# A different order for the start of an attention and expert layer: where the weights are staged, and when they are multiplied together

## The chip, the cores and the metric

The kernel runs on one NeuronCore of a Trainium2 chip. The metric is the time of one execution on the device, in microseconds; the figure before is the median of three runs. The engines are TensorE (PE; PEld are its weight loads), VectorE (DVE), ScalarE (ACT), GpSimd (POOL), and SyncE (SP), which issues all loads and stores. Each works through its own list of instructions in order; semaphores tie the lists together.

## What is computed

Eight batches of 128 rows and 512 columns, all float32. Per batch b:

```python
c  = x @ cond_weight[ids_b].T                 # a 512 x 512 matrix chosen by index
q, k, v = c @ Wq, c @ Wk, c @ Wv              # 32 heads of 16, 8 groups of k and v
ctx = softmax(causal(rope(q) @ rope(k).T / 4)) @ v
x1 = x + ctx @ Wo
c2 = x1 @ W.T + (x1 @ lora_A[id2_b]) @ lora_B.T / 2
base, logits, h = c2 @ W_base.T + b, c2 @ W_router.T, c2 @ A.T
w  = softmax over the two largest logits, zero elsewhere   # 8 experts
out = x1 + base + 2 * (h * w) @ B             # rank 16 for each expert
```

The second condition and what follows it have no nonlinearity between them. So the kernel multiplies their matrices once, at the start: `fused_w` = W.T times [router | A | base], 512 x 648, and `lora_g` = lora_B.T times the same. These products are made in ten *fusing blocks*.

## The kernel before

Every matrix operand is held as two halves, `hi` (rounded to fp32r) and `lo` (what is left), and a product takes three passes: hi hi, hi lo, lo hi. For weights ScalarE makes `hi` (a copy, L402) and VectorE makes `lo` (a subtraction, `low_of`, L588); for later batches' condition matrices GpSimd makes `lo` (L346). A weight thus goes through a load into a raw buffer, ScalarE, VectorE, and only then can TensorE use it. Weights of 512 rows come in KT = 4 quarters of 128.

Rounds. The work is software-pipelined. In round t, batch f = t + 1 is at its condition, projections and rotation, batch t at scores and softmax, r = t - 1 at context, output and FFN, q = t - 2 at its experts' end. The loop runs from t = -1, and each engine has its list written out as such a loop; the order in the list is the order of execution. The steps that matter here:

- `condition(f)`: 12 matmuls (L1020 to L1022). ScalarE copies the result (`copy_c`, tile turn), `transpose_c` turns it (L938), ScalarE and VectorE split it into c_t hi and lo (`split_c`), and `project_q` and `project_kv` use it (L927, L928, L932).
- ScalarE copies v out of PSUM (`copy_v`), VectorE multiplies q and k by the rotation's tables (`rotate_k`, `rotate_q`, L705, L707), GpSimd adds the two products (`add_rotated`, L362), `transpose_qk` turns them (L1047, L938), and ScalarE and VectorE split them (`split_qk`, `split_k`, `split_q`).
- `score(t, p)`, p = 0 to 3 (L954), is the first pass of scores, of which VectorE takes the row maxima (`maxima`, 8 instructions for each p, L655). p = 2 and 3 overwrite p = 0 and 1, so they wait until the maxima of those are read. `transpose_maxima` (L964) and `spread_maxima` bring the maxima into the second, transposed pass `score_t(t, e)` (L976, L981, L986), of which ScalarE takes the exponentials (`exp_scores`, L502).
- `fuse(n)`, n = 0 to 9 (L1133 to L1135): 12 matmuls of 324 columns into one of two PSUM banks in turn, drained by `split_fused(n)` on ScalarE and then VectorE. Blocks 0 and 1 make `lora_g`, 2 to 9 `fused_w`. A block can't start before the block two before it is drained. In the kernel before, all ten stand in round 0, each between two steps of batches 0 and 1. context(0, 0) of round 1 waits for the last drain.

Weights. w_q and w_kv are loaded first, into `stage_a`. FFN's matrices (router_t, experts_a_t, base_t) go to `stage_a` too, and SyncE issues them when the last quarter of q, k, v's is split (`qkv_lo`). w2 goes to `stage_b`, then w_o to the same. SyncE's list is: ids, x_t, w_kv; condition 0; w_q, cos and sin, w2, lora_b; batch 1's condition; FFN's, bias, experts_b, w_o; then batch by batch.

The exponentials of e = 0 are written over `stage_a`, those of e = 1 into a buffer of their own (`probs_1`).

## Time and profile before

| | us |
|---|---|
| median of 3 runs (268.58 to 269.58) | 268.69 |
| the profiled execution | 269.5 |
| its span, first to last instruction | 267.7 |
| TensorE busy in it | 237.8 |
| VectorE, ScalarE, GpSimd busy | 182.6, 117.9, 86.7 |
| mean granted clock of TensorE (1.0 is 2.4 GHz) | 0.974 |

The profile page gives shares of the whole span. For a change in the first 80 us the tables by stage and the engines' own timelines say more: a timeline's row gives start, duration, engine, line, operation, tile and count, and in brackets the idle time before it and what ended that. A matmul's duration holds some 0.17 us of pipeline behind its last column; the distance from start to start is its price.

### The profile page before, as it was taken

To read this page: it belongs to the slowest core of one execution; us is meant where nothing else is said; L and a number is where in the kernel's file an instruction comes from. 1 tells how busy PE (TensorE), PEld (TensorE's weight loads), DVE (VectorE), ACT (ScalarE), POOL (GpSimd) and SP (SyncE) were. 2 spreads that over 40 slices of the span, in tenths; PEclk is the share of its full clock that TensorE was granted. 3 is DMA by queue.
4 is the path that set the end of the run, shared out by engine and by line. 5 is a ranking of instruction groups with operands and counts; after the bars stand their busy time and mean duration, and the time that the engine had idled before them with its cause. 6 is when DMAs were issued, how large, how long until landed. Compare 5 with 4: busy or idle time off the path is not lost.

```text
span 267.7 us, 5712 instructions
## 1 busy us (share of the span) xinstructions
PE 237.8 (89%) x2010; PEld 176.8 (66%) x2010; DVE 182.6 (68%) x908; ACT 117.9 (44%) x269; POOL 86.7 (32%) x92
## 2 busy tenths in 40 slices
PE   0565699999699999999999999999999999889994
PEld 0444588888376866586658765876587766556883
DVE  3583766441985689668965896589658966977653
ACT  2687233457607443643364336433642164054210
POOL 7207405322928005610562056205620050001010
PEclk9988689999989999999999999999999999999999
DMA  5999340041000700260027001600200030001111
GB/s 140 329 349 380 141 139 0 2 164 36 0 12 7 232 2 1 69 218 2 1 61 224 5 1 59 229 0 4 63 28 0 4 76 15 0 4 42 46 42 39
DMA packets 20000, 21.17 MB, mean 79 GB/s; under 512 B 6404, under 2 KB 11524, under 8 KB 19972
## 3 DMA queue, kind: packets, MB, share of 16 engines
q1 hardware_dynamic: 19972, 20.81, 24.5%
q8 instruction: 16, 0.26, 0.4%
q14 instruction: 12, 0.10, 0.1%
HBM read 18.71 MB, written 2.10 MB: 78 GB/s over the span
## 4 chain that ended last, share of the span: by engine, by line
PE 63%; DVE 20%; issue 7%; ACT 6%; SPq 1%; DMA 1%; POOL 0%; DVEq 0%
PE bank L932 9%; PE bank L927 9%; PE bank L928 8%; DVE thrown L655 7%; PE bank L1006 4%; PE bank L954 3%; PE bank L1020 3%; PE bank L1078 3%; PE bank L1021 3%; PE bank L1022 3%; PE bank L938 3%; PE bank L1133 2%; PE bank L981 2%; DVE turned L673 2%; PE bank L1134 2%
## 5 line engine op out<-in xcount | busy, mean ns | idle before, releaser
L346 POOL TENSOR_TENSOR cond_w_lo<-cond_raw,cond_w_hi 128x512 fp32r<-128x512 f32 x28 | 36.3, 1310 | 69.7 <-ACT cond_w_hi L402 69.7
L655 DVE CUSTOM_DVE_ANT_0 thrown<-bank,causal 128x128 f32<-128x128 f32 x256 | 56.0, 283 | 0.0
L362 POOL TENSOR_TENSOR rope_b<-rope_a,rope_b 128x128 f32<-128x128 f32 (+1 forms) x16 | 16.2, 1015 | 52.9 <-DVE rope_b L707 52.9
L927 PE MATMUL bank<-qkv_w_hi,c_t_hi 128*128 128x512 f32 (+1 forms) x64 | 22.5, 368 | 1.4 <-DVE c_t_lo L588 1.4
L1020 PE MATMUL bank<-cond_w_hi,xt_hi 128*128 128x512 f32 x32 | 14.7, 459 | 9.4 <-DVE cond_w_lo L588 9.4
L928 PE MATMUL bank<-qkv_w_lo,c_t_hi 128*128 128x512 f32 (+1 forms) x64 | 21.7, 355 | 0.0
L927 PE MATMUL bank<-fused_w_hi,late 128*128 128x324 f32 (+2 forms) x68 | 20.9, 322 | 0.0
L655 DVE DVE_READ_ACCUMULATOR2_ANT neg_max<- 128x1 f32 x256 | 20.6, 81 | 0.0
L371 POOL TENSOR_TENSOR x_bias<-x,bias_row 128x512 f32<-128x512 f32 x8 | 10.2, 1278 | 29.9 <-DVE out_sb L809 28.8
L928 PE MATMUL bank<-fused_w_lo,late 128*128 128x324 f32 (+2 forms) x68 | 19.9, 306 | 0.0
L402 ACT ACTIVATE cond_w_hi<-cond_raw 128x512 fp32r<-128x512 f32 x32 | 17.8, 622 | 4.0 <-DMA cond_raw<-cond_w_t 4.0
L502 ACT ACTIVATE probs<-bank 128x512 f32<-128x512 f32 x32 | 16.5, 604 | 6.6 <-PE bank L986 6.6
L402 ACT ACTIVATE turn<-bank 128x512 f32<-128x512 f32 x8 | 4.8, 598 | 31.6 <-PE bank L1022 31.5
L927 PEld LDWEIGHTS bank<-qkv_w_hi,c_t_hi 128*128 128x128 f32 x64 | 12.7, 199 | 9.0 <-issue 5.8
L502 ACT ACTIVATE stage_a<-bank 128x512 f32<-128x512 f32 x32 | 16.5, 603 | 1.1 <-PE bank L986 0.3
L402 ACT ACTIVATE v_ones<-bank 128x64 f32<-128x64 f32 x16 | 2.7, 221 | 32.0 <-PE bank L932 32.0
L402 ACT ACTIVATE late<-bank 128x128 fp32r<-128x128 f32 (+1 forms) x24 | 9.5, 397 | 16.3 <-PE bank L1100 10.6
L954 PE MATMUL bank<-k_pad_hi,q_t_hi 32*128 32x256 f32 x128 | 11.2, 339 | 5.3 <-DVE neg_max L655 3.2
L402 ACT ACTIVATE max_rows<-bank,own_p 128x128 fp32r<-128x128 f32 x32 | 9.1, 373 | 11.8 <-PE bank L964 11.8
L1020 PEld LDWEIGHTS bank<-cond_w_hi,xt_hi 128*128 128x128 f32 x32 | 6.9, 217 | 11.2 <-issue 9.6
L932 PE MATMUL bank<-qkv_w_hi,c_t_lo 128*128 128x512 f32 (+1 forms) x64 | 14.3, 346 | 0.0
L1021 PE MATMUL bank<-cond_w_lo,xt_hi 128*128 128x512 f32 x32 | 14.3, 446 | 0.0
(150 smaller groups left out, 629.8 us busy)
## 6 DMA issues: line engine op xcount, KB each, us to landing
cond_raw<-cond_w_t SPq DMA_DIRECT2D x7, 1024.0 KB, 5.5
xt_raw<-x_t SPq DMA_DIRECT2D x8, 256.0 KB, 5.9
x_nat<-x SPq DMA_DIRECT2D x8, 256.0 KB, 2.6
out<-out_sb SPq DMA_DIRECT2D x8, 256.0 KB, 2.0
cond_raw<-cond_w_t SPq DMA_DIRECT2D x4, 256.0 KB, 3.6
stage_a<-w_q SPq DMA_DIRECT2D x4, 256.0 KB, 5.3
stage_b<-w SPq DMA_DIRECT2D x4, 256.0 KB, 4.9
stage_a<-base_t SPq DMA_DIRECT2D x1, 1024.0 KB, 7.4
```

The source lines that it names most:

```text
L346: pool.tensor_tensor(cond_w.lo[:, k, :], cond_raw[:, k, :], f32(cond_w.hi[:, k, :]), ALU.subtract).then_inc(cond_lo, 1)
L362: pool.tensor_tensor(qk[:, at:at + w], rope_a[:, at:at + w], rope_b[:, at:at + w], ALU.add).then_inc(qk_ready, 1)
L402: return nc.scalar.activation(out, in_, ACT.Copy, scale=scale)
L502: nc.scalar.activation(probs_t[e][j], s_ps[j][:, :], ACT.Exp).then_inc(exped, 1)
L655: nc.vector.tensor_tensor_reduce(thrown[:, p % 2, j, e, :], s_ps[j][:, at:at + P], causal[:, :], -1.0, -MASKED, ALU.add, ALU.min, neg_max[ ...
L927: nc.tensor.matmul(out, lhs.hi[:, k, :], rhs.hi[:, k, cols], start=(k == 0), stop=False)
L928: nc.tensor.matmul(out, lhs.hi[:, k, :], rhs.lo[:, k, cols], start=False, stop=False)
L932: mm = nc.tensor.matmul(out, lhs.lo[:, k, :], rhs.hi[:, k, cols], start=False, stop=(last and k == KT - 1))
L954: mm = nc.tensor.matmul(s_ps[j][:, at:at + 2 * P], query[tile_rows(j), p, :], key[tile_rows(j), :, :], start=(n == 0), stop=(n == 2))
L1006: mm = nc.tensor.matmul(ctx_ps(r, e)[tile_rows(j), :], v_ones[r % 2][e][:, j, :, :], probs_t[e][j], start=True, stop=True)
L1020: nc.tensor.matmul(y_ps[:, :], xt.hi[:, k, :], cond_w.hi[:, k, :], start=(k == 0), stop=False)
L1021: nc.tensor.matmul(y_ps[:, :], xt.hi[:, k, :], cond_w.lo[:, k, :], start=False, stop=False)
```

## The change

- FFN's raw weights get a buffer of their own, `stage_d`. It is the old `probs_1` made larger, and ctx_n takes its last 512 columns.
- SyncE's first loads are in another order: ids, x_t, lora_b, router_t, experts_a_t; condition 0; base_t in quarters; w2 in quarters; then w_kv and w_q by quarters; cos and sin. Batch 1's condition, bias and experts_b, w_o follow; w2 and base_t have a semaphore for each quarter.
- The splits of FFN, w2 and lora_b stand ahead of those of q, k, v's weights on ScalarE and VectorE, mixed with the steps of batch 0.
- Rounds -1 and 0 are written out on every engine, and the loop starts at t = 1. TensorE's list is shown below whole. Blocks 0 to 6 stand ahead of score(0, 0), block 7 behind condition(1), 8 and 9 in the second pass of batch 0's scores. transpose_maxima(0) waits for 8 drains instead of 4, since blocks now use c_ps until block 7; blocks 8 and 9 both use x_ps.
- `split_experts` goes from VectorE to GpSimd, behind `split_output`. On ScalarE `split_a(0)` now stands ahead of `split_output`.

```diff
...
+        stage_d = sb("stage_d", [P, KT * FFN])
...
-        probs_e = [stage_a, sb("probs_1", [P, KT * D])]
+        probs_e = [stage_a, stage_d]
...
-        ctx_n = sb("ctx_n", [P, D])
+        ctx_n = stage_d[:, KT * D:KT * D + D]
...
-        fused_ps = lambda n: (x_ps, c_ps)[n % 2][:, 0:HALF]
+        fused_ps = lambda n: (c_ps if n % 2 and n < 8 else x_ps)[:, 0:HALF]
...
-        ROUNDS = range(-1, BATCH - 1)
+        ROUNDS = range(1, BATCH - 1)
...
-                for k in range(KT):
-                    sp.dma_start(stage_qkv[:, k, D:QKV], w_kv[k * P:(k + 1) * P, :]).then_inc(qkv_in[k], 16)
+                sp.dma_start(lora_b_raw[:, :, :], lora_b.rearrange("(k p) r -> p k r", p=P)).then_inc(lb_in, 16)
+                for src, at in ((router_t, 0), (experts_a_t, EXPERTS)):
+                    sp.dma_start(stage_ffn[:, :, at:at + src.shape[1]], src.rearrange("(k p) n -> p k n", p=P)
+                                 ).then_inc(ffn_in, 16)
                 sp.wait_ge(ids_in, 32)
...
                 for k in range(KT):
+                    sp.dma_start(stage_ffn[:, k, GATES:FFN], base_t[k * P:(k + 1) * P, :]).then_inc(base_in[k], 16)
+                for k in range(KT):
+                    sp.dma_start(stage_b[:, k * D:(k + 1) * D], w2[k * P:(k + 1) * P, :]).then_inc(w2_in[k], 16)
+                for k in range(KT):
+                    sp.dma_start(stage_qkv[:, k, D:QKV], w_kv[k * P:(k + 1) * P, :]).then_inc(qkv_in[k], 16)
                     sp.dma_start(stage_qkv[:, k, 0:D], w_q[k * P:(k + 1) * P, :]).then_inc(qkv_in[k], 16)
...
             def later_weights():
-                sp.wait_ge(qkv_lo, KT)
...
             first_loads()
+            load_condition(1)
+            later_weights()
+            load_condition(2)
+            load_batch(0)
...
# GpSimd
+            def split_experts():
+                pool.wait_ge(b_hi, 1)
+                pool.tensor_tensor(moe_b.lo, stage_c[:, :], f32(moe_b.hi), ALU.subtract).then_inc(b_lo, 1)
...
+            for f in range(2):
+                split_condition(f + 1, 0)
+                split_condition(f + 1, 1)
+                add_rotated(f, rope_k, D, KV)
+                add_rotated(f, rope_q, 0, D)
+                split_condition(f + 1, 2)
+                split_condition(f + 1, 3)
+                split_xt(f + 1)
...
# ScalarE
             split_xt(0)
+            split_rank()
             split_condition(0, range(KT))
-            split_qkv()
+            split_ffn(0)
+            split_ffn(1)
+            split_ffn(2)
+            copy_c(0)
+            split_ffn(3)
+            split_c(0)
+            for k in range(KT):
+                split_second(k)
+            split_fused(0)
+            split_qkv(0)
+            split_qkv(1)
+            split_fused(1)
+            split_qkv(2)
+            split_qkv(3)
+            split_fused(2)
+            split_fused(3)
+            split_condition(1, range(2))
+            copy_v(0)
+            split_condition(1, range(2, KT))
+            split_fused(4)
+            split_xt(1)
+            split_fused(5)
+            split_qk(0)
+            split_fused(6)
...
# VectorE
             owns()
-            split_first()
+            for k in range(KT):
+                split_condition(k)
+            split_rank()
+            for k in range(KT):
+                split_ffn(k)
+            split_c(0)
+            for k in range(KT):
+                split_second(k)
+            split_fused(0)
+            split_qkv(0)
+            split_qkv(1)
+            split_fused(1)
+            split_qkv(2)
+            split_qkv(3)
+            sign_sin()
+            split_fused(2)
+            split_fused(3)
+            rotate_k(0)
+            rotate_q(0)
+            split_fused(4)
+            split_fused(5)
+            split_k(0)
+            split_q(0)
+            split_fused(6)
+            dve.wait_ge(tables_made, 2)
+            maxima(0, 0)
+            maxima(0, 1)
+            split_fused(7)
+            split_c(1)
...
# TensorE
                 if n >= 2:
-                    pe.wait_ge(fused_lo, n - 1)
-                if n == 5:
-                    pe.wait_ge(max_spread, 1)
+                    pe.wait_ge(fused_lo, n - 1 if n < FUSED - 1 else n)
...
+            condition(0)
+            transpose_c(0)
+            fuse(0)
+            fuse(1)
+            fuse(2)
+            fuse(3)
+            project_q(0)
+            project_kv(0)
+            fuse(4)
+            fuse(5)
+            transpose_qk(0)
+            fuse(6)
+            score(0, 0)
+            score(0, 1)
+            condition(1)
+            fuse(7)
+            transpose_c(1)
+            score(0, 2)
+            score(0, 3)
+            project_q(1)
+            project_kv(1)
+            transpose_maxima(0)
+            score_t(0, 0)
+            fuse(8)
+            transpose_qk(1)
+            score_t(0, 1)
+            fuse(9)
+            score(1, 0)
+            score(1, 1)
             for t in ROUNDS:
...
```

## Rows read from the trace of the kernel before

**Rows 1.** Busy time by stage: TensorE, weight loads, VectorE, ScalarE, GpSimd, clock, DMA

```profile
...
14.90:23.70 8.80, 6.69 (x28) 5.29 (x28) 4.98 (x9) 6.62 (x12) 3.14 (x3) 0.81 1.09 350
23.70:30.10 6.40, 0.77 (x5) 0.55 (x6) 3.16 (x10) 4.09 (x9) 4.82 (x5) 0.87 0.59 220
30.10:36.20 6.10, 6.09 (x36) 4.96 (x37) 6.10 (x37) 0.00 (x0) 0.00 (x0) 0.57 0.80 262
36.20:65.70 29.50, 29.50 (x270) 26.20 (x269) 12.61 (x58) 15.59 (x37) 8.52 (x8) 1.00 0.15 48
65.70:80.00 14.30, 12.15 (x96) 7.65 (x94) 12.07 (x79) 5.94 (x13) 9.35 (x8) 0.88 0.03 6
...
110.00:240.00 130.00, 124.64 (x1130) 88.85 (x1130) 98.15 (x536) 55.99 (x136) 40.10 (x36) 1.00 0.17 52
...
```

**Rows 2.** TensorE's timeline, 17 to 80 us

```profile
...
17.64 0.50 PE L927 MATMUL bank<-qkv_w_hi,c_t_hi 128*128 128x512 f32 x1 [1.41 <-DVE c_t_lo L588]
...
27.29 0.33 PE L1047 MATMUL bank<-ident,rope_b 128*128 128x128 f32 x1 [3.62 <-POOL rope_b L362]
...
30.11 0.59 PE L954 MATMUL bank<-k_pad_hi,q_t_hi 32*128 32x256 f32 x4 [2.05 <-DVE q_t_lo L737]
...
43.09 0.40 PE L927 MATMUL bank<-qkv_w_hi,c_t_hi 128*128 128x512 f32 x1
...
45.90 0.31 PE L1133 MATMUL bank<-shared,late 128*128 128x324 f32 x1
...
58.85 0.43 PE L976 MATMUL bank<-later_b,ident_b 32*32 32x512 bf16 x16
...
60.35 0.41 PE L1133 MATMUL bank<-shared,late 128*128 128x324 f32 x1
...
64.08 0.39 PE L954 MATMUL bank<-k_pad_hi,q_t_hi 32*128 32x256 f32 x4
...
64.99 0.50 PE L1020 MATMUL bank<-cond_w_hi,xt_hi 128*128 128x512 f32 x1
...
71.78 0.39 PE L954 MATMUL bank<-k_pad_hi,q_t_hi 32*128 32x256 f32 x4 [2.15 <-DVE neg_max L655]
...
79.58 0.27 PE L964 MATMUL bank<-ident,max_cols 128*128 128x128 f32 x1
...
```

**Rows 3.** ScalarE's timeline, 0 to 80 us

```profile
...
7.92 1.27 ACT L402 ACTIVATE cond_w_hi<-cond_raw 128x512 fp32r<-128x512 f32 x2 [3.04 <-DMA cond_raw<-cond_w_t]
...
16.90 2.19 ACT L402 ACTIVATE late<-stage_b 128x512 fp32r<-128x512 f32 x4
...
```

**Rows 4.** VectorE's timeline, 0 to 80 us

```profile
...
12.26 3.77 DVE L588 TENSOR_TENSOR qkv_w_lo<-stage_a,qkv_w_hi 128x768 fp32r<-128x768 f32 x4 [0.39 <-ACT qkv_w_hi L402]
...
17.56 2.50 DVE L588 TENSOR_TENSOR late<-stage_b,late 128x512 fp32r<-128x512 f32 x4
...
29.88 3.06 DVE L588 TENSOR_TENSOR shared<-stage_a,shared 128x648 fp32r<-128x648 f32 x4
...
46.64 0.49 DVE L588 TENSOR_TENSOR fused_w_lo<-bank,fused_w_hi 128x324 fp32r<-128x324 f32 x1
...
67.26 1.07 DVE L588 TENSOR_TENSOR shared<-stage_c,shared 128x512 fp32r<-128x512 f32 x1 [2.10 <-ACT shared L402]
...
```

**Rows 5.** GpSimd's timeline, 0 to 80 us

```profile
...
65.22 5.47 POOL L352 TENSOR_TENSOR shared<-stage_b,shared 128x512 fp32r<-128x512 f32 x4 [9.89 <-ACT shared L402]
...
```

**Rows 6.** DMA issues from 0 to 50 us: count, KB each, median us to landing

```profile
...
cond_raw<-cond_w_t SPq DMA_DIRECT2D x4, 256.0 KB, 3.6
...
stage_a<-experts_a_t SPq DMA_DIRECT2D x1, 256.0 KB, 5.3
...
lora_b_raw<-lora_b SPq DMA_DIRECT2D x1, 64.0 KB, 5.4
...
stage_a<-router_t SPq DMA_DIRECT2D x1, 16.0 KB, 4.8
...
```

**Rows 7.** Busy time microsecond by microsecond, columns as in rows 1

```profile
...
19.00:20.00 1.00, 1.00 (x4) 0.80 (x3) 1.00 (x3) 0.76 (x3) 0.00 (x0) 0.50 1.24 263
...
```

More of the change, by code:

```diff
@@ L176, in build_program @@
         cond_first_in = [sem(f"cond_first_in{k}") for k in range(KT)]
-        o_in, w2_in, ffn_in, b_in, lb_in = sem("o_in"), sem("w2_in"), sem("ffn_in"), sem("b_in"), sem("lb_in")
+        w2_in = [sem(f"w2_in{k}") for k in range(KT)]
+        base_in = [sem(f"base_in{k}") for k in range(KT)]
+        o_in, ffn_in, b_in, lb_in = sem("o_in"), sem("ffn_in"), sem("b_in"), sem("lb_in")
         out_free = sem("out_free")
@@ L279, in first_loads @@
                 sp.dma_start(rope_sin[:, :], sin[0:P, :]).then_inc(tables_in, 16)
-                for k in range(KT):
-                    sp.dma_start(stage_b[:, k * D:(k + 1) * D], w2[k * P:(k + 1) * P, :]).then_inc(w2_in, 16)
-                sp.dma_start(lora_b_raw[:, :, :], lora_b.rearrange("(k p) r -> p k r", p=P)).then_inc(lb_in, 16)
             def later_weights():
-                sp.wait_ge(qkv_lo, KT)
-                stage_ffn = stage_a[:, 0:KT * FFN].rearrange("p (k n) -> p k n", k=KT)
-                for src, at in ((router_t, 0), (experts_a_t, EXPERTS), (base_t, GATES)):
-                    sp.dma_start(stage_ffn[:, :, at:at + src.shape[1]], src.rearrange("(k p) n -> p k n", p=P)
-                                 ).then_inc(ffn_in, 16)
                 sp.dma_start(bias_row[:, :], base_bias.partition_broadcast(P)).then_inc(bias_in, 16)
@@ L379, in _ @@
                     split_output()
+                    split_experts()
                 if prep:
@@ L414, in split_condition, with split_qkv, split_rank, split_second @@
                     copy(cond_w.hi[:, k, :], cond_raw[:, k, :]).then_inc(cond_hi, 1)
[L416 to L424 removed]
+            def split_qkv(k):
+                act.wait_ge(qkv_in[k], 32)
+                copy(qkv_w.hi[:, k, :], stage_a[:, k * QKV:(k + 1) * QKV]).then_inc(qkv_hi, 1)
+            def split_rank():
                 act.wait_ge(lb_in, 16)
                 copy(lora_bw.hi[:, :, :, :], four_times(lora_b_raw)).then_inc(lb_hi, 1)
[L428 to L431 removed]
+            def split_second(k):
+                act.wait_ge(w2_in[k], 16)
+                copy(w2_w.hi[:, k, :], stage_b[:, k * D:(k + 1) * D]).then_inc(w2_hi, 1)
+            def split_ffn(k):
+                act.wait_ge(ffn_in, 32)
+                act.wait_ge(base_in[k], 16)
+                copy(ffn_w.hi[:, k, :], stage_d[:, k * FFN:(k + 1) * FFN]).then_inc(ffn_hi, 1)
             def split_fused(n):
@@ L495, in exp_scores @@
             def exp_scores(t, e):
-                if t == 0 and e == 0:
-                    act.wait_ge(ffn_lo, KT)
+                if t == 0:
+                    act.wait_ge((qkv_lo, ffn_lo)[e], KT)
                 if t > 0:
@@ L512, in _ @@
             split_xt(0)
+            split_rank()
             split_condition(0, range(KT))
-            split_qkv()
+            split_ffn(0)
[22 more added lines that the diff above has]
+            split_fused(6)
+            copy_c(1)
+            split_fused(7)
+            split_c(1)
+            split_condition(2, range(KT))
+            split_xt(2)
+            copy_v(1)
+            spread_maxima(0)
+            exp_scores(0, 0)
+            split_qk(1)
+            split_fused(8)
+            exp_scores(0, 1)
+            split_fused(9)
+            split_a(0)
+            split_output()
             for t in ROUNDS:
@@ L641, in split_fused @@
                            ).then_inc(fused_lo, 1)
-            def split_experts():
-                dve.wait_ge(b_hi, 1)
-                low_of(moe_b.lo, stage_c[:, :], moe_b.hi).then_inc(b_lo, 1)
             def maxima(t, p):
@@ L812, in _ @@
             owns()
-            split_first()
+            for k in range(KT):
[25 more added lines that the diff above has]
+            maxima(0, 1)
+            split_fused(7)
+            split_c(1)
+            maxima(0, 2)
+            maxima(0, 3)
+            split_maxima(0)
+            rotate_k(1)
+            rotate_q(1)
+            split_k(1)
+            split_q(1)
+            split_fused(8)
+            split_fused(9)
             for t in ROUNDS:
@@ L1159, in _ @@
                     transpose_c(f)
-                if t == 0:
-                    fuse(1)
                 if batch(t):
@@ L1164, in _ @@
                     score(t, 3)
-                if t == 0:
-                    fuse(2)
                 if batch(q):
@@ L1181, in _ @@
                     score_t(t, 0)
-                if t == 0:
-                    fuse(5)
                 if batch(r):
@@ L1194, in _ @@
                     score_t(t, 1)
-                if t == 0:
-                    fuse(8)
-                    fuse(9)
                 if batch(r):
@@ L1200, in _ @@
                     project_ffn(r, 0, left_ps(r)).then_inc(gates_done, 1)
-                if t >= 0 and batch(f):
+                if batch(f):
                     score(f, 0)
```

105 lines of the change are left out of this document (17 added, 88 removed).

## The prediction

> **What bounds the kernel now.** I read the stages first. From 110 to 240 us TensorE is busy 124.64 of 130 us at full clock [rows 1], so the later rounds run at TensorE's pace, and a change in the first two rounds moves all that follows by what it saves there. In the stages before 80 us the same table shows two kinds of loss: TensorE stands idle (busy 6.69 of 8.80 us, then 0.77 of 6.40, later 12.15 of 14.30), and it runs at the lower of its two levels (mean granted clock 0.81, 0.57, 0.88 in three of the stages; 1.0 is 2.4 GHz, 0.5 is 1.2 GHz). From 36.2 to 65.7 us it is busy 29.50 of 29.50 us: this is where the ten fusing blocks stand between the steps of batches 0 and 1, and nothing is lost there.
>
> Next I read TensorE's own timeline for the places where it waits [rows 2]: 1.41 us before the first projection (the halves of c_t), 3.62 us before the transposes of q and k (copy of v, rotation on VectorE, addition on GpSimd), 2.05 us before the first scores (splitting q and k), and 2.15 us before score(1, 2), for the maxima. That last wait starts on VectorE: it ends `split_experts`, a 1.07 us subtraction that had waited 2.10 us for ScalarE, at 68.3 us [rows 4], although score(1, 1) was complete at about 65.0 [rows 2]. The maxima of batch 1 thus start 3.3 us late; 16 of them fill the 3.45 us to 71.78. Behind it the clock falls for a stretch.
>
> So between 14.9 and 79.58 us, TensorE loses 9.2 us idle in the four named places. To lower clock it loses half of each low stretch in which it works: (1 - 0.81) x 8.8 = 1.7, (1 - 0.57) x 6.1 = 2.6 and (1 - 0.88) x 14.3 = 1.7 us, 6.0 in all. Each is a low stretch of about 3.4 us of work, the middle one longer. The most that a reordering of the start can give is some 15 us.
>
> **The change, part by part.** No arithmetic is added or removed. Prices: a fusing block costs (64.08 - 60.35) / 2 = 1.87 us at full clock [rows 2], so 13.1 for seven; at the low clock an estimated 3.7 (twice). The projection of q takes 45.90 - 43.09 = 2.81 us at full clock [rows 2]; that of k and v has half the columns, 1.41. A pair of scores takes 64.99 - 64.08 = 0.91, a whole score_t 60.35 - 58.85 = 1.50.
>
> Loads. SyncE now issues three small loads instead of four of w_kv ahead of the first condition's, so these may be issued a little sooner. But two of the three consist of short runs (32 bytes for the router, 128 for lora_b). In the trace of before, the microsecond in which router and experts were in flight moved 263 GB/s against 350 in its stage [rows 1, 7]: some 0.25 us lost. At the other end, if each held the queues for its whole time to landing (5.4, 4.8, 5.3 us [rows 6]), it would be 15.5 us. Those times were measured behind megabytes of other loads, so I take the near end, and as fewer bytes stand ahead than with w_kv, I count neither gain nor loss. After the condition, base_t, w2 and the projections' weights follow, 3.7 MB; at 350 GB/s [rows 1] their last land 3, 6 and 10.5 us behind the condition's (itself at about 10 us), that is 13, 16 and 20.5. ScalarE wants them at about 14, 16.7 and 22. Cover is 0.7 us at the narrowest; what is lost if it is gone is the lateness itself. Batch 1's condition is now issued behind them, lands at about 24 and is wanted at 25. FFN's weights no longer wait until stage_a has been read.
>
> The Trainium skill, DMA: Bandwidth & Descriptors (Specifications, and Rules for kernel authors), speaks against this step: transfers want runs of 512 bytes or more, and under 64 KB one pays mostly overhead; router_t is 16 KB in 32-byte runs. With the page's fixed cost of about 2 us (fitted there for the DMAs that GpSimd issues) paid three times in a row, an estimate by that page is a start 6 us later and a gain of some 4.5 us in place of 10.7. The row of the 263 GB/s speaks against it.
>
> First projection. The transposes of c(0) end at 17.64 - 1.41 = 16.2 us, as before. From there VectorE is the chain: the last FFN quarter 3.06 / 4 = 0.77, c_t's low half 0.69, w2 2.50, a drain 0.49, two quarters of qkv 1.88, a drain 0.49, two quarters 1.88 [rows 4]: 8.7 us, and project_q(0) starts at about 25.0, where it was at 17.6. ScalarE's share of a quarter of w2 is 0.55 [rows 3] against VectorE's 0.62, the wider quarters in proportion, so it stays ahead. TensorE meanwhile does fuse(0) to fuse(3), 7.5 us of work in 8.8 us, with gaps under 1 us: before fuse(2), for w2 and the first drain, and before fuse(3), whose drain stands behind two quarters of qkv on VectorE. Here I choose that the clock stays up. If it falls for one stretch as long as the first of before, 3.4 us, it costs 1.7, of which the gaps hide about 1.
>
> Then q and k and v at full clock, 4.2: until 29.2. fuse(4) and fuse(5), 3.7, lie in the 3.62 us wait for the rotated q and k: transposes at about 33.0. fuse(6), 1.87, lies in the 2.05 us wait behind them: first scores at 35.85 (30.11 before), ended at 36.8. GpSimd, behind the addition for q at 33.0, still has three subtractions of batch 1 at about 1.3 us [rows 5]; condition(1) starts at 36.9 and ends at 39.7 at full clock.
>
> From there, before took from 36.2 to 64.99, 28.8 us, always busy. Seven blocks less makes 15.7. Three new waits come in, since there is less to cover with: 0.55 before project_q(1) (the 1.41 path, with one pair of scores over it), 0.3 before the maxima's spread, and 1.0 before fuse(9), whose drain waits behind splitting q and k on ScalarE and VectorE (2.05 + 0.49 against one score_t of 1.50). Condition(2) then starts at 39.7 + 15.7 + 1.85 = 57.2 instead of 65.0: **7.8 us saved**.
>
> Round 1. `split_experts` goes from VectorE to GpSimd (1.3 to 1.4 us there [rows 5], beside work that isn't wanted for 10 us; b_lo is wanted a round later). VectorE is free when score(1, 1) is there, and 3.45 us of maxima fit beside condition(2), context and transposes, 4.6 us: the **2.15 us** wait goes. Without that idle time the low clock behind it goes too, 1.6; but VectorE (context turned, c_t, scale, 16 maxima) then is what transpose_maxima(1) waits for, some 0.6 later than TensorE: **1.0 us**. That step is at 79.58 in the trace of before. Everything behind it moves as one.
>
> Sum: 7.8 + 2.15 + 1.0 = 10.95, with no start gain counted. The execution profiled took 269.5 (span 267.7, 1.8 around it); by its own account 258.55 comes of it. It lies 0.8 above the median of 268.69, so the median after is 257.75; rounded up for hand-overs not counted, **258.0**. The likeliest case's own range is 256.3 to 259.5: the start gain and a condition(0) that warms earlier at one end, an error of 1.5 in some twenty steps at the other.
>
> **Rivals.**
> - *The clock falls in the new start* once or twice (chance 0.20). For it: it fell before after idle stretches in this very place, and there will be four or five gaps of up to 1 us. Against: from 23.7 to 30.1 us TensorE worked 0.77 of 6.40 us, and the granted clock was still 0.87 over that stage [rows 1]. Price 1.7 for each, less what is hidden: 259.5 to 261.4.
> - *Weights late* (0.10): base_t or w2 land 2 us behind my reckoning, and VectorE's chain with them. 260.
> - *Round 1 gives nothing* (0.10): another wait, on GpSimd's longer queue or ScalarE's `split_output` ahead of copy_c(2), takes the place of the one for the maxima; 3.15 less saved, 261.1.
> - *Not faster* (0.05): the short-run loads hold the first condition back. Everything hangs on that load, so lateness counts in full; from 10.7 us on there is no gain. At the far bound they hold the queues from 1.9 to 17.4 us, and the first quarter, 3.6 us to its landing [rows 6], comes at 21.0 instead of 7.9 [rows 3]: 271.1. The trace's 263 GB/s speaks against it.
> - *Better than forecast* (0.10): VectorE's chain and the start are both a little shorter, 255 to 256.3.
> - *The forecast*: 0.45.
>
> A difference under 0.5%, 1.3 us, can't be told from no change here. From the cases: faster 0.95, within it 0.02, slower 0.03. The range takes in the forecast and its neighbours up to two falls of the clock: 255.8 to 261.5.
>
> **What would show it.** In the profile after: project_q(0) at about 25, behind a VectorE that is busy without a break from 16 us; waits of 3.62 and 2.05 us gone or under 0.5; condition(1) at 37, condition(2) at 57; no idle time for the maxima of batch 1; granted clock 1.0 from 15 to 80 us. Wrong it would be by a first matmul much later than 9.4 us, by ScalarE waiting for loads between 10 and 22 us, or by low clock in the fusing blocks.

## The result, and the profile after

| | before | after |
|---|---|---|
| median, us | 268.63 (267.76 to 269.58, 4 runs) | 258.88 (258.01 to 259.66, 4 runs) |
| the profiled execution | 269.5 | 259.66 |
| its span | 267.7 | 257.9 |
| mean granted clock | 0.974 | 0.998 |

The medians differ by 9.7 us. The ratio of the runs beside each other is 0.9612, with a 95% interval of 0.9578 to 0.9647; of 268.6 us that is 10.4 us, 9.5 to 11.3. Forecast were 258.0 and a range of 255.8 to 261.5. Beside the experiments the kernel before took 267.7 to 271.6 us, more where its mean clock was lower (0.962 to 0.980).

First the busy time by stage of the changed kernel, columns as in [rows 1] (stretch, its length, then TensorE, weight loads, VectorE, ScalarE, GpSimd, clock, DMA share, GB/s).

```profile
...
14.90:23.70 8.80, 7.01 (x45) 6.52 (x46) 7.48 (x11) 7.88 (x14) 0.00 (x0) 1.00 1.07 368
23.70:30.10 6.40, 6.40 (x40) 5.70 (x39) 2.48 (x8) 2.26 (x7) 2.53 (x2) 1.00 0.58 214
30.10:36.20 6.10, 5.73 (x49) 5.23 (x51) 3.80 (x11) 3.55 (x9) 5.09 (x5) 1.00 0.00 0
36.20:57.00 20.80, 19.36 (x202) 15.55 (x198) 12.19 (x83) 11.43 (x27) 8.45 (x8) 1.00 0.25 83
57.00:69.00 12.00, 11.73 (x104) 7.75 (x96) 10.69 (x75) 7.15 (x16) 10.64 (x9) 1.00 0.31 108
...
102.00:232.00 130.00, 123.94 (x1154) 88.62 (x1154) 98.12 (x536) 56.07 (x136) 37.87 (x35) 1.00 0.16 52
...
```

From 14.9 to 36.2 us TensorE was busy 13.55 of 21.3 us before, at a clock down to 0.57 [rows 1]; now it is busy 19.14 us, and every row of the table reads 1.00. The later rounds are as they were: 123.94 of 130 us busy here, 124.64 before [rows 1]. Next TensorE's timeline, to be held against [rows 2].

```profile
...
15.48 0.66 PE L985 MATMUL bank<-ident,turn 128*128 128x128 f32 x4 [0.69 <-ACT turn L421]
...
20.60 0.39 PE L1178 MATMUL bank<-shared,late 128*128 128x324 f32 x1 [0.92 <-DVE lora_g L624]
...
22.89 0.41 PE L1178 MATMUL bank<-shared,late 128*128 128x324 f32 x1 [0.28 <-DVE lora_g L624]
...
24.84 0.47 PE L974 MATMUL bank<-qkv_w_hi,c_t_hi 128*128 128x512 f32 x1
...
32.93 0.33 PE L1094 MATMUL bank<-ident,rope_b 128*128 128x128 f32 x1
...
35.74 0.39 PE L1001 MATMUL bank<-k_pad_hi,q_t_hi 32*128 32x256 f32 x4 [0.26 <-DVE q_t_lo L769]
...
43.35 0.50 PE L974 MATMUL bank<-qkv_w_hi,c_t_hi 128*128 128x512 f32 x1 [0.50 <-DVE c_t_lo L624]
...
54.66 0.42 PE L1178 MATMUL bank<-shared,late 128*128 128x324 f32 x1 [0.85 <-DVE fused_w_lo L624]
...
57.55 0.50 PE L1067 MATMUL bank<-cond_w_hi,xt_hi 128*128 128x512 f32 x1
...
62.09 0.39 PE L1001 MATMUL bank<-k_pad_hi,q_t_hi 32*128 32x256 f32 x4
...
69.36 0.33 PE L1011 MATMUL bank<-ident,max_cols 128*128 128x128 f32 x1 [0.55 <-DVE max_cols L697]
...
```

The waits of 3.62, 2.05 and 2.15 us of [rows 2] are gone: the transposes of q and k (32.93) and score(1, 2) (62.09) stand there without a bracket, and the first scores (35.74) wait 0.26 us. Three other waits are new, 0.92 before fuse(2), 0.50 before project_q(1) and 0.85 before fuse(9). transpose_maxima(1) comes at 69.36 instead of 79.58, 10.2 us earlier; the last transpose_maxima comes at 224.8 instead of 234.7, the end of the span at 257.9 instead of 267.7, 9.8 earlier.

VectorE's timeline shows what paces the new start, and one row to keep for later.

```profile
...
16.09 0.83 DVE L624 TENSOR_TENSOR shared<-stage_d,shared 128x648 fp32r<-128x648 f32 x1 [1.20 <-ACT shared L421]
16.85 0.68 DVE L624 TENSOR_TENSOR c_t_lo<-bank,c_t_hi 128x512 fp32r<-128x512 f32 x1
17.45 2.48 DVE L624 TENSOR_TENSOR late<-stage_b,late 128x512 fp32r<-128x512 f32 x4
19.96 0.49 DVE L624 TENSOR_TENSOR lora_g<-bank,lora_g 32x324 fp32r<-32x324 f32 x1
20.49 1.83 DVE L624 TENSOR_TENSOR qkv_w_lo<-stage_a,qkv_w_hi 128x768 fp32r<-128x768 f32 x2
22.35 0.49 DVE L624 TENSOR_TENSOR lora_g<-bank,lora_g 32x324 fp32r<-32x324 f32 x1
22.87 1.82 DVE L624 TENSOR_TENSOR qkv_w_lo<-stage_a,qkv_w_hi 128x768 fp32r<-128x768 f32 x2
...
62.82 0.69 DVE L624 TENSOR_TENSOR c_t_lo<-bank,c_t_hi 128x512 fp32r<-128x512 f32 x1 [0.47 <-ACT c_t_hi L421]
...
63.71 1.05 DVE L714 TENSOR_TENSOR scaled<-turned,inv_sum 128x256 f32<-128x256 f32 x1
...
69.50 0.42 DVE L714 TENSOR_TENSOR scaled<-turned,inv_sum 128x256 f32<-128x256 f32 x1
...
```

From 16.09 to 24.69 us VectorE has no idle time at all. GpSimd's timeline around 60 us has the moved step behind `split_output`:

```profile
...
58.20 5.04 POOL L358 TENSOR_TENSOR shared<-stage_b,shared 128x512 fp32r<-128x512 f32 x4 [3.07 <-ACT shared L421]
63.21 1.27 POOL L363 TENSOR_TENSOR shared<-stage_c,shared 128x512 fp32r<-128x512 f32 x1
...
```

And ScalarE's shows the loads: the first condition's quarter is taken at 7.83 us (7.92 before [rows 3]), and base_t is waited for 0.15 us.

```profile
...
7.83 1.26 ACT L421 ACTIVATE cond_w_hi<-cond_raw 128x512 fp32r<-128x512 f32 x2 [2.25 <-DMA cond_raw<-cond_w_t]
...
11.49 2.08 ACT L421 ACTIVATE shared<-stage_d 128x648 fp32r<-128x648 f32 x3 [0.15 <-DMA stage_d<-base_t]
...
```

### The profile page after: what moved, and what is told of

Its sections match the earlier page's. It is cut to its first block, busy times and chain, and to the rows that moved or that the text cites. A ratio compares the mean times of both kernels' runs of the same rounds, so it can differ in the third digit from the quotient of the medians.

```text
span 257.9 us, 5719 instructions
## 1 busy us (share of the span) xinstructions
PE 232.9 (90%) x2010; PEld 173.1 (67%) x2010; DVE 182.1 (71%) x907; ACT 117.7 (46%) x269; POOL 87.6 (34%) x93
## 3 DMA queue, kind: packets, MB, share of 16 engines
q1 hardware_dynamic: 20020, 20.81, 24.7%
## 4 chain that ended last, share of the span: by engine, by line
PE 58%; DVE 23%; issue 8%; ACT 7%; DMA 1%; SPq 1%; POOL 1%; DVEq 0%; ACTq 0%
PE bank L974 9%; PE bank L979 8%; PE bank L975 7%; DVE thrown L687 7%; PE bank L1067 3%; PE bank L1053 3%; PE bank L1125 3%; PE bank L1069 3%; PE bank L1068 3%; PE bank L1001 3%; DVE late L624 3%; DVE turned L705 3%; PE bank L985 2%; PE bank L1028 2%; ACT k_pad_hi L421 2%
## 5 line engine op out<-in xcount | busy, mean ns | idle before, releaser
L1067 PE MATMUL bank<-cond_w_hi,xt_hi 128*128 128x512 f32 x32 | 13.9, 433 | 9.3 <-DVE cond_w_lo L624 9.3
L974 PE MATMUL bank<-qkv_w_hi,c_t_hi 128*128 128x512 f32 (+1 forms) x64 | 21.4, 352 | 0.6 <-DVE c_t_lo L624 0.5
L687 DVE DVE_READ_ACCUMULATOR2_ANT neg_max<- 128x1 f32 x256 | 20.8, 81 | 0.0
L975 PE MATMUL bank<-qkv_w_lo,c_t_hi 128*128 128x512 f32 (+1 forms) x64 | 20.5, 336 | 0.0
L381 POOL TENSOR_TENSOR x_bias<-x,bias_row 128x512 f32<-128x512 f32 x8 | 10.2, 1280 | 29.9 <-DVE out_sb L841 28.9
L521 ACT ACTIVATE stage_d<-bank 128x512 f32<-128x512 f32 x32 | 16.5, 603 | 5.6 <-PE bank L1033 5.5
L974 PEld LDWEIGHTS bank<-qkv_w_hi,c_t_hi 128*128 128x128 f32 x64 | 12.0, 188 | 7.8 <-issue 4.2
L624 DVE TENSOR_TENSOR late<-bank,late 128x512 fp32r<-128x512 f32 (+1 forms) x16 | 7.8, 489 | 9.0 <-ACT late L421 9.0
L974 PE MATMUL bank<-shared,late 128*128 128x512 f32 x32 | 13.1, 409 | 1.1 <-issue 0.7
```

Source lines behind the costliest of these rows:

```text
L381: pool.tensor_tensor(x1_bias[:, :], x1[:, :], bias_row[:, :], ALU.add).then_inc(x1b_ready, 1)
L521: nc.scalar.activation(probs_t[e][j], s_ps[j][:, :], ACT.Exp).then_inc(exped, 1)
L624: return nc.vector.tensor_tensor(lo, value, f32(hi), ALU.subtract)
L687: nc.vector.tensor_tensor_reduce(thrown[:, p % 2, j, e, :], s_ps[j][:, at:at + P], causal[:, :], -1.0, -MASKED, ALU.add, ALU.min, neg_max[ ...
L974: nc.tensor.matmul(out, lhs.hi[:, k, :], rhs.hi[:, k, cols], start=(k == 0), stop=False)
L975: nc.tensor.matmul(out, lhs.hi[:, k, :], rhs.lo[:, k, cols], start=False, stop=False)
```

## The experiments

Each ran beside the kernel before on the same chip; a ratio is to that, with its 95% interval in brackets. Where two ratios are compared, 0.01 is 2.7 us. Where "the trace" is said, the place is transpose_maxima(1), behind which all moves as one: 79.58 us before, 69.36 after. The intervals of the ratios are some 0.003 to 0.007 wide to either side, 1 to 2 us, so that for differences under 1 us the traces say more than the times.

**`split_experts` back on VectorE, the rest of the change kept.**

```diff
# GpSimd
                     split_output()
-                    split_experts()
# VectorE
             split_fused(9)
+            split_experts()
```

> The changed kernel with split_experts back on VectorE, behind the last fusing drain; all else as changed. Theory (round 1's 3.15 us come from this move): VectorE waits for ScalarE's experts copy until 60.2 us, subtracts until about 61.2, and starts the maxima of batch 1 there instead of at 57.7. score(1, 2) comes at 64.7 instead of 62.1, TensorE idles about 2.6 us before it, and the low clock may follow: slower by 2.6 to 3.6 us, about 262. Rival (the reordering alone had removed that wait, the move is worth nothing): within 0.5 us of the changed kernel.

Measured: 262.64 us (261.90 to 262.97), ratio 0.9754 [0.9683, 0.9824], where the change has 0.9612: 3.8 us of the gain are lost. VectorE, then TensorE, then the stage that was low in [rows 1]:

```profile
...
60.39 1.06 DVE L619 TENSOR_TENSOR shared<-stage_c,shared 128x512 fp32r<-128x512 f32 x1 [2.52 <-ACT shared L416]
...
```

```profile
...
64.90 0.39 PE L1001 MATMUL bank<-k_pad_hi,q_t_hi 32*128 32x256 f32 x4 [2.57 <-DVE neg_max L686]
...
```

```profile
...
65.70:80.00 14.30, 13.87 (x118) 9.17 (x114) 10.69 (x53) 5.45 (x15) 7.75 (x8) 0.88 0.06 9
...
```

All of what the prediction said of this step is back: VectorE idle for ScalarE (2.52, 2.10 in [rows 4]), the wait for the maxima (2.57, 2.15 in [rows 2]), and the low clock behind it (0.88). transpose_maxima(1) comes at 72.68, 3.3 us later than with the whole change; the prediction's term for it was 3.15. The two waits are 0.4 us longer than in the kernel before because `split_a(0)` now stands ahead of `split_output` on ScalarE, so that 0.4 of this price belongs to the changed order.

**That step alone, in the kernel before.**

```diff
# GpSimd
                 if t == 1:
                     split_output()
+                    split_experts()
# VectorE
                     split_fused(9)
-                    split_experts()
```

> The kernel before with only split_experts moved to GpSimd behind split_output. Theory: maxima of batch 1 start at about 65.0 instead of 68.3, the 2.15 us idle time before score(1, 2) and the low clock behind it go; 3.15 us faster than before, 265.5, with the maxima's end then about 0.6 us behind TensorE. Rival (another wait takes its place: VectorE's chain behind is what binds): 1.5 us faster or less. Second rival: GpSimd, behind in its queue, delays condition(3) in round 2: no gain at all.

Measured: 266.74 us (265.56 to 268.09, 10 runs), ratio 0.9910 [0.9874, 0.9947], a gain of 2.2 us. In TensorE's timeline score(1, 2) waits no more, and

```profile
...
65.43 0.50 PE L1020 MATMUL bank<-cond_w_hi,xt_hi 128*128 128x512 f32 x1
...
76.83 0.33 PE L964 MATMUL bank<-ident,max_cols 128*128 128x128 f32 x1 [0.44 <-DVE max_cols L666]
...
```

transpose_maxima(1) is 2.75 us earlier than in [rows 2]. But condition(2) starts at 65.43 here and at 64.99 there: this execution is 0.44 us behind before anything runs that the edit touches. Its granted clock was 1.00, 0.69 and 0.50 in the three stages from 14.9 to 36.2 us, where [rows 1] have 0.81, 0.87 and 0.57. From condition(2) to transpose_maxima(1) it takes 11.40 us instead of 14.59, 3.19 less. This is the prediction's term 2.15 + 1.0 = 3.15 measured by itself, and it is right. The 2.2 us of the medians have an interval of 1.4 to 3.4. VectorE's timeline has a row to keep for later:

```profile
...
71.62 0.61 DVE L683 TENSOR_TENSOR scaled<-turned,inv_sum 128x256 f32<-128x256 f32 x1
...
```

**The idle places filled with useless work instead of blocks.** In the kernel before, 38 bf16 matmuls of 384 columns on constants go into a bank that is not in use; they leave what is computed as it is. No step is moved ahead by it, so it gives what the clock alone is worth.

```diff
+            def fill(n):
+                for _ in range(n):
+                    nc.tensor.matmul(x_ps[:, 0:D - P], ident_b[:, :], later_b[:, 0:PAIRS - 1, :], start=True, stop=True)
...
                     transpose_c(f)
+                if t == -1:
+                    pe.wait_ge(owns_made, 7)
+                    fill(7)
...
                     project_kv(f)
+                if t == -1:
+                    fill(20)
...
                     transpose_qk(f)
+                if t == -1:
+                    fill(11)
```

> The kernel before with matmuls of no use (bf16, 384 columns, about 0.16 us each at full clock, into the bank that block 0 will overwrite) in the waits of round -1: 7 behind transpose_c(0), 20 behind project_kv(0), 11 behind transpose_qk(0). The results stay the same. It keeps TensorE at work without doing anything sooner, and so shows what of the gain is clock alone. Theory (the low stretches follow from idle time): no low stretch from 15 to 36 us, project_q/kv(0) up to 1.7 us shorter and scores with condition(1) up to 2.5 us shorter: 264.5 to 265.5. Rival (the clock is low there for another reason, or the fill gets in the way): low stretches stay, time as before or up to 1 us more.

Measured: 266.44 us (266.14 to 266.80), ratio 0.9895 [0.9826, 0.9964], a gain of 2.5 us; 264.5 to 265.5 was expected. The clock did what was wanted, but not all of it arrived:

```profile
...
30.10:36.20 6.10, 6.10 (x52) 5.42 (x48) 6.07 (x39) 1.32 (x3) 0.00 (x0) 1.00 0.82 269
...
```

This stage had 0.57 in [rows 1]. The first scores come at 29.70 instead of 30.11 only, although q, k and v were projected at full clock. GpSimd's timeline shows why:

```profile
...
21.31 3.75 POOL L346 TENSOR_TENSOR cond_w_lo<-cond_raw,cond_w_hi 128x512 fp32r<-128x512 f32 x3 [13.18 <-ACT cond_w_hi L402]
25.02 1.71 POOL L362 TENSOR_TENSOR rope_b<-rope_a,rope_b 128x128 f32<-128x128 f32 x2
...
```

The addition for k has no bracket: GpSimd went to it straight from the third subtraction of batch 1's condition, where it waited for VectorE before. A faster projection runs into GpSimd's queue. So the clock alone gives 2.5 us of the 9.7 in this place; what work in the idle places gives is the next run's question.

**Only four blocks ahead.** The changed kernel with blocks 4 to 6 behind condition(1), among the steps of batches 0 and 1.

```diff
# TensorE; the drains on ScalarE and VectorE move likewise
             project_kv(0)
-            fuse(4)
-            fuse(5)
             transpose_qk(0)
-            fuse(6)
             score(0, 0)
             score(0, 1)
             condition(1)
-            fuse(7)
+            fuse(4)
             transpose_c(1)
+            fuse(5)
             score(0, 2)
             score(0, 3)
+            fuse(6)
             project_q(1)
+            fuse(7)
             project_kv(1)
```

> The changed kernel with only blocks 0 to 3 ahead of the first scores; 4 to 6 stand behind condition(1), among the steps of batches 0 and 1, where the kernel before had them. Theory (blocks 4 to 6 are worth what the waits of 3.62 and 2.05 us hide): both waits return, the first scores stay at 35.8, 5.5 us of blocks come behind them, of which some 1.0 us fill the waits before project_q(1) and fuse(9): 4 to 5 us slower than the changed kernel, and up to 2 more if the clock falls over the wait: 263 to 265. Rival (the early position alone does it, the number of blocks ahead matters little): slower by less than 2 us.

Measured: 266.36 us (265.56 to 268.16, 10 runs), ratio 0.9900 [0.9871, 0.9929]: 7.7 us of the gain are gone, more than the 4 to 7 that were expected. TensorE's timeline, then its stages:

```profile
...
33.08 0.47 PE L1094 MATMUL bank<-ident,rope_b 128*128 128x128 f32 x1 [3.61 <-POOL rope_b L372]
...
36.45 0.59 PE L1001 MATMUL bank<-k_pad_hi,q_t_hi 32*128 32x256 f32 x4 [2.05 <-DVE q_t_lo L769]
...
```

```profile
...
30.10:36.20 6.10, 1.33 (x5) 0.93 (x5) 2.69 (x9) 2.40 (x6) 4.89 (x5) 0.62 0.00 0
36.20:57.00 20.80, 20.55 (x165) 17.66 (x165) 10.94 (x80) 6.76 (x17) 3.35 (x4) 0.87 0.26 81
```

The two waits are the 3.62 and 2.05 of [rows 2] to 0.01 us: they are paths through other engines, and blocks 4 to 6 fill them without making them longer. Three blocks are 5.6 us; the rest is the low clock, (1 - 0.87) x 20.8 = 2.7 us, less what the wait before project_q(1), absent here, gives back. The ratio that is left, 0.9900, is that of the moved step alone (0.9910): the first four blocks ahead gain next to nothing by themselves (condition(2) starts at 65.36 us, at 64.99 before), and it is the three in the two waits that pay.

**The three small loads behind the first condition's.**

```diff
-                sp.dma_start(lora_b_raw[:, :, :], ...)
-                for src, at in ((router_t, 0), (experts_a_t, EXPERTS)): ...
                 sp.wait_ge(ids_in, 32)
...
+                # the same three, between condition 0 and base_t
# ScalarE
-            split_rank()
             split_condition(0, range(KT))
+            split_rank()
```

> The changed kernel with the three loads of short runs (lora_b, router, experts' A) issued behind the first condition's four quarters instead of ahead, and lora_b's split behind the condition's on ScalarE. Theory (they cost little): first matmul at 9.34 us comes 0.3 to 1.0 us sooner, 0.2 to 1.0 us faster. Rival (the page's rule: mostly overhead, about 2 us each): first matmul 3 us sooner or more, some 3 us faster; at the other end the FFN quarters, now behind them, come late and nothing is gained.

Measured: 258.58 us (258.38 to 258.81), ratio 0.9608 [0.9541, 0.9675], not to be told from the change's 0.9612. ScalarE's timeline:

```profile
...
5.99 1.28 ACT L421 ACTIVATE cond_w_hi<-cond_raw 128x512 fp32r<-128x512 f32 x2 [1.15 <-DMA cond_raw<-cond_w_t]
...
11.47 2.04 ACT L421 ACTIVATE shared<-stage_d 128x648 fp32r<-128x648 f32 x3 [1.40 <-DMA stage_d<-base_t]
...
13.89 0.60 ACT L421 ACTIVATE turn<-bank 128x512 f32<-128x512 f32 x1 [0.38 <-PE bank L1069]
...
```

The condition is there 1.8 us sooner (5.99 against 7.83), but base_t is not: ScalarE takes it at 11.47, in the changed kernel at 11.49. TensorE's timeline:

```profile
...
8.57 0.77 PE L1067 MATMUL bank<-cond_w_hi,xt_hi 128*128 128x512 f32 x1 [8.57 <-POOL xt_lo L347]
...
```

The first matmul starts at 8.57, 0.8 earlier, and now waits for GpSimd's `xt_lo`: that takes back 1.1 of the 1.8 us. base_t takes back nothing here, since the copy of the condition's result (13.89) waits for TensorE and not for ScalarE's work on base_t. transpose_maxima(1) comes at 68.4, 1.0 earlier than in the profiled execution of the change and 0.5 earlier than in a second one (68.9). So the three loads together hold the first condition by 1.8 us, and cost the kernel at most 1. The Trainium skill, DMA: Bandwidth & Descriptors (Anatomy of one DMA), gives about 2 us of fixed cost to one transfer. The prediction's estimate added three of them, a start 6 us later. This run disagrees with adding them up: behind one another in a queue, three transfers held the next by 1.8 us in all.

**w2 ahead of base_t.** The two loops of SyncE's first loads change places.

> The changed kernel with w2 loaded ahead of base_t. base_t's quarters come 2.9 us later. Theory (base_t has hardly any slack, 0.15 us of waiting in the changed kernel's trace already): ScalarE's copy_c(0) stands behind the third quarter, which lands at about 15.4, so it starts at 16.1 instead of 14.8, and the whole chain is 1.2 to 1.5 us later: 260.2. Rival (there are slack and covers enough): less than 0.5 us.

Measured: 261.19 us (260.62 to 261.55), ratio 0.9693 [0.9644, 0.9743]: 2.2 us slower than the change, more than the 1.2 to 1.5 that were expected. ScalarE's timeline and TensorE's stage:

```profile
...
14.93 2.06 ACT L421 ACTIVATE shared<-stage_d 128x648 fp32r<-128x648 f32 x3 [2.80 <-DMA stage_d<-base_t]
...
```

```profile
...
14.90:23.70 8.80, 6.18 (x33) 6.18 (x34) 7.82 (x12) 8.03 (x15) 0.00 (x0) 0.81 1.07 370
...
```

base_t is taken 3.4 us later. ScalarE's copy_c(0), `turn`, stands behind it, so TensorE waits 2.68 us before transpose_c(0), and its clock falls. The first scores come 2.0 us later. Of the 3.4 us, 1.4 are absorbed: in the changed kernel ScalarE has nothing to do for 1.26 us before copy_c(0). This is the rival "weights late", made on purpose: the order of these loads has 1.4 us of slack here and no more.

**The drain of block 8 ahead of the splits of q and k.**

```diff
# ScalarE
             exp_scores(0, 0)
+            split_fused(8)
             split_qk(1)
-            split_fused(8)
             exp_scores(0, 1)
# VectorE
             rotate_q(1)
+            split_fused(8)
             split_k(1)
             split_q(1)
-            split_fused(8)
             split_fused(9)
```

> The changed kernel with block 8's drain ahead of the splitting of q and k of batch 1, on ScalarE and on VectorE. Theory: block 8 is complete at 51.8 us and ScalarE is free at 51.93, so the drain is over at 52.9 instead of 54.6; fuse(9) follows score_t(0, 1) with no gap, and the 0.85 us wait before it goes: 0.7 to 0.9 us faster than the changed kernel. Rival: k and q of batch 1 are split 0.4 us later and score(1, 0) or the exponentials wait in its place: no difference.

Measured: 258.50 us (257.89 to 258.70), ratio 0.9596 [0.9558, 0.9633], 0.4 us better than the change by ratio, less than the intervals can tell. TensorE's timeline has no wait before fuse(9) and instead one before score(1, 0):

```profile
...
55.87 0.39 PE L1001 MATMUL bank<-k_pad_hi,q_t_hi 32*128 32x256 f32 x4 [0.33 <-ACT stage_d L521]
...
```

Scores 35.53 (0.2 earlier than after), transpose_maxima(1) 68.22 (1.1 earlier): 0.9 us between the two places.

**GpSimd takes three subtractions of VectorE's chain** (quarter 1 of w2, quarters 0 and 2 of w_q, w_kv), since it is idle from 8 to 26 us.

```diff
# GpSimd
             split_xt(0)
+            pool.wait_ge(w2_hi, 2)
+            pool.tensor_tensor(w2_w.lo[:, 1, :], stage_b[:, D:2 * D], f32(w2_w.hi[:, 1, :]), ALU.subtract).then_inc(w2_lo, 1)
+            for k in (0, 2):
+                pool.wait_ge(qkv_hi, k + 1)
+                pool.tensor_tensor(qkv_w.lo[:, k, :], ...).then_inc(qkv_lo, 1)
```

> The changed kernel with three of VectorE's twelve weight subtractions (quarter 1 of w2, quarters 0 and 2 of q, k, v's) on GpSimd, which is idle there from 8.1 to 26 us. Theory (VectorE's list sets project_q(0)): its list loses 2.5 us, ScalarE's copies and the blocks then bind, project_q(0) starts at about 23.9 instead of 24.84: 0.7 to 0.9 us faster than the changed kernel. Rival (the two engines slow each other when both read and write the same memory, as the 1.07 us against 0.69 of the same subtraction in the trace of before hints): VectorE's subtractions take 0.9 to 1.1 us for 0.62 and nothing is gained, or up to 0.5 us is lost.

Measured: 259.26 us (258.92 to 259.83), ratio 0.9632 [0.9595, 0.9670]: nothing gained, though VectorE has 2.5 us less to do. VectorE's timeline, then GpSimd's:

```profile
...
17.47 2.08 DVE L631 TENSOR_TENSOR late<-stage_b,late 128x512 fp32r<-128x512 f32 x2 [0.24 <-ACT late L428]
...
20.10 1.95 DVE L631 TENSOR_TENSOR qkv_w_lo<-stage_a,qkv_w_hi 128x768 fp32r<-128x768 f32 x1
...
```

```profile
...
19.10 4.64 POOL L390 TENSOR_TENSOR qkv_w_lo<-stage_a,qkv_w_hi 128x768 fp32r<-128x768 f32 x2 [0.70 <-ACT qkv_w_hi L428]
...
```

The 2.08 us are two quarters of w2: 1.47 for the first, beside GpSimd's subtraction, and 0.6 for the second. One quarter of w_q, w_kv takes VectorE 1.95 us, longer than two (1.83) when GpSimd is idle. A new question came of it: is it the buffers that both read, or the two engines at work at once?

**GpSimd kept busy on constants.** The changed kernel with six additions of 128 by 512 on GpSimd that read only the identity and write a buffer that is rewritten later; nothing that is computed changes.

```diff
# GpSimd
             split_xt(0)
+            pool.wait_ge(w2_hi, 1)
+            same = ident[:, :].unsqueeze(1).broadcast_to([P, KT, P])
+            for i in range(6):
+                if i > 0:
+                    pool.wait_ge(spun, i)
+                pool.tensor_tensor(view, same, same, ALU.add).then_inc(spun, 1)
```

> The changed kernel with six additions of no use on GpSimd (128x512, into x1_bias, which nothing reads yet) from about 17.2 us on, while VectorE splits the weights of w2 and of q, k, v. They touch none of VectorE's buffers. Theory (e6 gained nothing because the two engines slow each other at SBUF, whatever the buffers): VectorE's subtractions take 1.0 us for 0.62 and up to 1.95 for 0.94 while an addition runs, project_q(0) comes 3 to 5 us later: 262 to 264. Rival (e6's cost was that both worked on the same buffers, or the hand-overs): VectorE keeps its 0.62 and 0.94, the time stays within 0.5 us of e9; GpSimd is free again before it is wanted at 25.3.

Measured: 264.13 us (263.22 to 264.77), ratio 0.9791 [0.9738, 0.9844]; the changed kernel itself, on the same chip (below), had 259.11. VectorE, then GpSimd:

```profile
...
17.57 5.86 DVE L633 TENSOR_TENSOR late<-stage_b,late 128x512 fp32r<-128x512 f32 x4
...
```

```profile
...
17.49 8.54 POOL L392 TENSOR_TENSOR x_bias<-ident 128x512 f32<-128x512 f32 x6 [9.35 <-ACT late L430]
...
```

Four subtractions that take 2.48 us after take 5.86 here, 1.46 each, with 1.42 for each of GpSimd's: they go in step, one and one. No buffer is common to both, so it is the engines' access to the memory that they share, and not a buffer. TensorE waits 4.29 us for `lora_g`, and the clock falls to 0.59 in the stage behind.

**The changed kernel again, and a combination.** The second takes the small loads behind the condition and block 8's drain first, and lets GpSimd do `split_xt(0)` ahead of its memsets, since with an earlier condition the first matmul waited for `xt_lo`.

> The changed kernel itself, run once more as the standard beside e10 and e11 on the same chip. All theories: 258 to 260, with project_q(0) at about 25 us and the same five short waits before 60 us.

> The changed kernel with e4's order of loads and e5's order of block 8's drain together, and GpSimd's split of x_t(0) ahead of its buffer clearing, since the first matmul of e4 waited for it (8.57 us). Theory (the three savings add up, each as its trace showed: 0.95 from the start, 0.5 to 0.85 from the drain): first matmul at about 7.5 us, but ScalarE still waits for base_t until about 11.5, so nothing more than 0.4 comes of the third edit; 1.4 to 2.0 us faster than the changed kernel. Rival (each was noise, or base_t's landing gives all of it back): within 0.5 us of e9.

Measured on one chip: the changed kernel 259.11 us (258.76 to 259.57, 6 runs), ratio 0.9616 [0.9577, 0.9656], so the gain of the change came a second time; the combination 257.51 us (257.09 to 258.24, 6 runs), ratio 0.9562 [0.9522, 0.9602]. The runs of the two don't overlap, and the combination is 1.6 us faster than the changed kernel. It is the best of all that ran. Its first matmul starts at 8.26, its transpose_maxima(1) at 67.2. That is only 0.3 us ahead of the run with the small loads moved (8.57, for `xt_lo`). VectorE's timeline and GpSimd's show why:

```profile
...
5.60 1.92 DVE L642 CAST later_b<-thrown 128x512 bf16<-128x512 f32 x1
...
```

```profile
...
5.50 1.30 POOL L348 TENSOR_TENSOR xt_lo<-xt_raw,xt_hi 128x512 fp32r<-128x512 f32 x1
...
```

The conversion, 0.72 us in the changed kernel, takes 1.92 beside GpSimd's subtraction, and the condition's first `lo` stands behind it. base_t now counts too, but little: copy_c(0) follows ScalarE's work on it without a gap, and TensorE's wait before transpose_c(0) is 0.83 us instead of 0.69.

## Why the prediction was right, step by step

The forecast was 258.0; 258.88 came, inside the likeliest case's own range (256.3 to 259.5). None of the rivals is needed.

| step | forecast | measured |
|---|---|---|
| project_q(0) | 25.0 | 24.84 |
| transposes of q and k | 33.0 | 32.93 |
| first scores | 35.85 | 35.74 |
| condition(1) | 36.9 | 36.72 |
| the three new waits | 0.55, 0.3, 1.0 | 0.50, none listed, 0.85 |
| condition(2) | 57.2 (7.8 saved) | 57.55 (7.4 saved) |
| condition(2) to transpose_maxima(1) | 3.15 saved | 2.8 saved (3.2 by itself) |
| there | 10.95 saved | 10.2 saved |
| end of the span | 10.95 saved | 9.8 saved |

- **The new start.** VectorE is the chain from 16 to 24.7 us, priced at 8.7 and measured at 8.6. The fall of the clock, the largest rival, did not come: the gaps are 0.69, 0.92 and 0.28 us, and the clock stayed at 1.00. With a gap of 2.68 it fell (w2 ahead of base_t), and with one of 4.29.
- **Loads.** No gain or loss was counted; the quarter came 0.1 us sooner. That the small loads cost next to nothing was nearly right: they hide a condition that could land 1.8 us earlier, but the first matmul then waits for `xt_lo`, which takes back 1.1 of that. ScalarE's wait of 0.15 us for base_t was not in the reckoning, which gave the loads a cover of 0.7; it cost nothing, since ScalarE was idle again before copy_c(0). At the very start executions of one kernel differ by as much: in the changed kernel's second trace the first matmul is 0.6 us later (9.93), but its matmuls stand 0.43 us apart only up to 12.6 us and 0.23 from there, and transpose_c(0) is 0.4 us earlier (15.04 against 15.48).
- **Covering the waits with blocks.** Shown by the run with four blocks ahead, where exactly the two waits come back.
- **From condition(1) to condition(2).** Forecast 20.3, measured 20.83. The waits are 0.5 shorter than forecast and the stretch is still 0.5 longer, so 28.8 - 13.1 was too small by about 1 us. The two timelines, step by step from start to start, show where. Without blocks and waits the steps took 10.3 us before and take 11.0 now: transpose_c(1) 0.53 for 0.35, the transposes of q and k 0.64 for 0.47, score_t(0, 0) 1.86 for 1.74, the rest less each. And the ten blocks took 18.4 us before and the three that are left take 5.6, so that seven were worth 12.8 and not 13.1. These are the hand-overs that the prediction did not count; why they are dearer without a block beside them was not tried. That the forecast of condition(2) is only 0.4 us off is in part luck, since the 0.5 on the waits goes the other way.
- **Round 1.** The term 2.15 + 1.0 is right alone (3.19) and 0.4 too large in the whole change (2.8). With the whole change VectorE's own list runs unbroken from 62.8 us to the transpose, and in it `scaled` takes 1.05 us (1.03 in the changed kernel's second trace). It took 0.54 before and 0.61 with the moved step alone, and the next one takes 0.42. In the whole change it stands almost wholly beside the moved `split_experts` (63.21 to 64.48); alone, the step ended at 71.95, a third into `scaled`. So the cost at nothing that I gave GpSimd's work, "beside work that isn't wanted for 10 us", is what failed. GpSimd's own time was covered; what it takes from VectorE was not looked at. That the engines hinder one another was shown by the two runs above; that these 0.4 us are what is missing here is read from the rows, not tried.
- **The last 0.4 us**, from 10.2 to 9.8, are lost over the rounds from transpose_maxima(1) to the end. They are of the size by which traces differ there anyway: from transpose_maxima(1) to the last one it takes 155.1 us before, 155.4 after, and 154.9 to 155.6 in the experiments.

By the medians the two halves of the change gain 2.2 us (the moved step) and 6.3 (the new start, 268.96 to 262.64) by themselves, and 9.7 together. That does not show that the moved step is worth more in the changed kernel: the intervals leave room for 1 us and more, and from condition(2) to transpose_maxima(1) the step saves 3.19 us in the kernel before and 3.16 in the changed one (14.97 without it, 11.81 with it).

## What to carry to other kernels

Independent work that must be done once is best spent where TensorE waits for a path through other engines; the length of that path can be read from the wait before, and it stays the same when it is filled. A step given to another engine is free only when that engine's list has room, and when it does not stand beside work of the first engine that uses the same memory: look at what the two do at the same moment. And a first matmul behind a load is as early as its latest operand: when one load came 1.8 us sooner, GpSimd's `xt_lo` and then a conversion on VectorE were what it waited for.

## What the hardware showed that I had not expected

- **VectorE and GpSimd slow one another when both read two operands from SBUF.** A 128 by 512 subtraction on VectorE takes 0.62 us alone, 1.46 and 1.47 beside one of GpSimd's operations; one of 128 by 768 takes 0.92 alone and 1.95 beside one. GpSimd loses less: 1.42 where it has 1.26 to 1.27. When one of VectorE's operands comes from PSUM nothing happens: `c_t_lo` takes 0.69 us at 62.82, beside GpSimd's `split_output` and `split_experts`, and 0.68 with GpSimd idle. The Trainium skill, SBUF — State Buffer (Who interferes with whom), says that a VectorE instruction with two SBUF inputs contends with a GpSimd instruction that reads SBUF, and that one with at most one SBUF input, outside its 2-port modes, does not. The runs agree with both. The page calls the shared port pair an exclusive lock, and says of VectorE's 2-port modes that the instruction that issues later fully blocks. By full blocking an estimate would be 0.62 + 1.27 = 1.89 us for a pair of these subtractions; the measured 1.46 lies below it, so that the two overlap in part. The conversion in the combination (one input, from SBUF) does what full blocking would give: GpSimd's subtraction ends at 6.80, and the conversion at 7.52, its own 0.72 us later.
- **Useless bf16 matmuls hold the clock as well as real ones**, where TensorE is idle otherwise: the granted clock is 1.00 in every stage from 14.9 to 57 us, where 0.57 to 1.00 was granted before.
- **Small loads in front of a large one are cheap.** 336 KB in three loads, two of them in runs of 32 and 128 bytes, held the next load back by 1.8 us; 336 KB at the 350 GB/s of [rows 1] are 1.0 us by themselves.
